# Attention part: value products of two steps together in even steps, projection pieces of two steps together in odd steps, three probability buffers

## What is computed

```python
xn = layernorm(x)                                       # each row
# attention on xn (its own layer norm inside)
q, k, v = proj(Wq, bq), proj(Wk, bk), proj(Wv, bv)      # (8, 16, 1024, 16)
q, k = rope(q), rope(k)
attn = softmax(q @ k.T / sqrt(16))                      # 1024 x 1024 for each of 128 heads
a = xn + (attn @ v).reshape(8, 1024, 256) @ Wo.T + bo
# experts on xn: each of 8 experts takes the 256 rows of a batch with the highest affinity
f = scatter_add(gating * (silu(xs @ Wg) * (xs @ Wu)) @ Wd)
out = x + a + f
```

## Time and profile before

| | us |
|---|---|
| median of 3 runs (2110.39 to 2111.07) | 2110.73 |
| time of the profiled execution | 2107.77 |
| its span, first to last instruction | 2106.2 |
| PE busy | 1842.3 |
| ACT busy | 1197.9 |
| DVE busy | 1113.1 |
| mean granted TensorE clock | 0.949 |

### The profile page before, as it was taken

The page is one execution under the profiler, slowest core; times in us unless marked ns, Lnnn a source line. Parts: engine busy times, 40 slices in busy tenths (PEclk is TensorE's granted clock), DMA queues, the critical chain, the costliest instruction groups (busy, mean ns, idle before and its releaser), DMA issues. The chain is left out here.

```text
span 2106.2 us, 31941 instructions
## 1 busy us (share of the span) xinstructions
PE 1842.3 (87%) x11244; PEld 1004.2 (48%) x11245; DVE 1113.1 (53%) x1904; ACT 1197.9 (57%) x1390; POOL 659.3 (31%) x599
## 2 busy tenths in 40 slices
PE   2469989989989989989989998964999888888997
PEld 2323423423423433334333332224887777777876
DVE  8745446446536536446545558963444444444543
ACT  0058768778778777768867887852333332332331
POOL 3323123123113113212212210001655545455554
PEclk9779999989989999989999999986999999999999
DMA  2255355364363474464464454323433434244333
GB/s 89 84 119 113 94 126 135 103 138 123 100 157 98 116 163 97 126 153 105 127 142 102 127 119 100 77 68 110 88 52 82 76 56 90 45 87 78 55 58 41
DMA packets 115707, 211.63 MB, mean 100 GB/s; under 512 B 17600, under 2 KB 55872, under 8 KB 115520
## 3 DMA queue, kind: packets, MB, share of 16 engines
q1 hardware_dynamic: 84032, 150.33, 29.4%
q0 software_dynamic: 31488, 58.74, 13.6%
HBM read 116.22 MB, written 92.80 MB: 99 GB/s over the span
## 5 line engine op out<-in xcount | busy, mean ns | idle before, releaser
L553 ACT ACTIVATE probs<-score 128x1024 f32<-128x1024 f32 x1024 | 989.0, 1023 | 332.2 <-PE score L708 326.9
L679 PE MATMUL o_ps<-probs,v_ones 128*32 128x512 f32 x4096 | 563.6, 623 | 11.2 <-DVE o_sb L939 10.6
L708 PE MATMUL score<-q_stack,k_stack 50*128 50x512 f32 x2048 | 428.3, 474 | 50.8 <-issue 26.9
L708 PEld LDWEIGHTS score<-q_stack,k_stack 50*128 50x128 f32 x2048 | 184.6, 189 | 308.6 <-issue 166.0
L1220 POOL DMA_INDIRECT out<-y,rows_now x128 | 202.5, 1582 | 268.5 <-DVE y L1372 231.8
L1259 ACT ACTIVATE silu<-g_ps 128x512 f32<-128x512 f32 x128 | 76.5, 598 | 360.9 <-PE g_ps L1293 343.3
L487 POOL TENSOR_TENSOR square<-qk 128x512 bf16<-128x512 f32 x64 | 87.3, 1393 | 475.3 <-DVE qk L858 475.3
L1361 DVE TENSOR_TENSOR h<-u_ps,silu 128x512 f32<-128x512 f32 x128 | 88.5, 692 | 212.3 <-PE u_ps L1293 181.6
L679 PEld LDWEIGHTS o_ps<-probs,v_ones 128*32 128x32 f32 x4096 | 81.6, 109 | 167.7 <-issue 153.2
L1211 POOL DMA_INDIRECT xs<-xn_rows,rows_now x128 | 130.9, 1023 | 47.6 <-issue 29.2
L939 DVE COPY o_sb<-o_ps 128x512 f32<-128x512 f32 x64 | 44.1, 688 | 158.5 <-PE o_ps L679 158.5
(11 more groups left out here) (138 smaller groups left out, 2984.4 us busy)
## 6 DMA issues: line engine op xcount, KB each, us to landing
q_parts<-parts SPq DMA_DIRECT2D x16, 1024.0 KB, 4.4
k_parts<-parts SPq DMA_DIRECT2D x16, 1024.0 KB, 8.2
q_stack<-q_parts SPq DMA_DIRECT2D x64, 256.0 KB, 6.9
k_stack<-k_parts SPq DMA_DIRECT2D x64, 256.0 KB, 8.6
o_sums<-o_sb SPq DMA_DIRECT2D x64, 256.0 KB, 4.8
xin<-in_x POOLq DMA_DIRECT2D x16, 512.0 KB, 5.4
xn_rows<-xn POOLq DMA_DIRECT2D x16, 512.0 KB, 4.9
out<-xin POOLq DMA_DIRECT2D x16, 512.0 KB, 3.4
```

The lines of the kernel that those rows point to most:

```text
L553: act.activation(probs[s % 2][:, 2 * i:2 * i + 2, :], score[i][:, :, :], ACT.Exp, scale=SCALE).then_inc(exp_done[i], 1)
L679: last = pe.matmul(o_ps[j * KEYS_W:(j + 1) * KEYS_W, :], v_ones[par][:, kt, j, :], probs[s % 2][:, j, :], start=kt == 0, stop=kt == KT - 1)
L708: last = pe.matmul(score[i][:, w, :], k_stack[par][rows, i, kt * P:(kt + 1) * P], q_stack[par][rows, i, qh * HALF:(qh + 1) * HALF], start= ...
```

## The change

The order of issue on TensorE changes within each pair of steps (an even and the following odd one). In an even step TensorE issues the scores and then the value products of the two steps before. In an odd step it issues the scores and then all pieces that the tables give to either step of the pair. The tables themselves stay. So pieces of an even step come one step later, and value products of an even step one step later, too. The transposes of affinities at the start of batch 7 stay in step 0, behind the value products. `probs` gets a third buffer; `probs_of` names the buffer of a step, with an extra turn at step 51 so that 64 steps close the cycle, and `steps_since` the distance to the last use of it, which ScalarE's wait on `pv_done` now uses. At the end two steps' value products remain. VectorE, GpSimd and SyncE keep their programs.

```diff
@@ -163,7 +163,7 @@
     q_stack = [sb(f"q_stack{i}", [P, NPAIR, S], F32R) for i in range(2)]
     k_stack = [sb(f"k_stack{i}", [P, NPAIR, S], F32R) for i in range(2)]
     v_ones = [sb(f"v_ones{i}", [P, KT, HPG, KEYS_W]) for i in range(2)]
-    probs = [sb(f"probs{i}", [P, HPG, HALF]) for i in range(2)]
+    probs = [sb(f"probs{i}", [P, HPG, HALF]) for i in range(3)]
     row_max = sb("row_max", [P, HPG * KT])
     neg_max = sb("neg_max", [HPG * KT, P])
     shift = sb("shift", [HPG * KT, NPART, P], F32R)
@@ -237,6 +237,8 @@
                    (39, 40, 41), (42, 43, 44), (45, 46, 47), (48, 49, 50), (56, 57)))
     V_STEPS = ((51, 51, 52), (52, 53, 53), (54, 54, 55), (57, 58, 58))
     PEAK_STEP = (60, 61)
+    EXTRA_STEP = 51
+    assert EXTRA_STEP % 3 == 0 and (STEPS - 1 - EXTRA_STEP) % 3 == 0
     WO_STEPS = ((11, 12, 13), (14, 15, 16), (40, 41, 42), (43, 44, 45))
 
     NORM_STEP, ROUTER_STEP, AFFINITY_STEP = (2, 15), (15, 39), (18, 42)
@@ -250,6 +252,14 @@
     def in_order():
 
         return sorted(((th, k) for th in range(2) for k in range(HJOBS)), key=lambda tk: JOB[tk[0]][tk[1]])
+
+    def probs_of(s):
+
+        return s % 3 if s < EXTRA_STEP else 1 if s == EXTRA_STEP else (s - EXTRA_STEP - 1) % 3
+
+    def steps_since(s):
+
+        return next(n for n in range(1, STEPS) if probs_of((s - n) % STEPS) == probs_of(s))
 
     def need(eng, s, value):
 
@@ -549,8 +559,8 @@
                 for i in range(2):
                     act.wait_ge(qk_done[i], at + 1)
                     if i == 0:
-                        need(act, pv_done, at - 1)
-                    act.activation(probs[s % 2][:, 2 * i:2 * i + 2, :], score[i][:, :, :], ACT.Exp,
+                        need(act, pv_done, at - steps_since(s) + 1)
+                    act.activation(probs[probs_of(s)][:, 2 * i:2 * i + 2, :], score[i][:, :, :], ACT.Exp,
                                    scale=SCALE).then_inc(exp_done[i], 1)
                 if nxt is not None and s in ROUTER_STEP:
                     router(nxt, ROUTER_STEP.index(s))
@@ -677,7 +687,7 @@
                 pe.wait_ge(v_ones_ready, group + 1)
             for j in range(HPG):
                 last = pe.matmul(o_ps[j * KEYS_W:(j + 1) * KEYS_W, :], v_ones[par][:, kt, j, :],
-                                 probs[s % 2][:, j, :], start=kt == 0, stop=kt == KT - 1)
+                                 probs[probs_of(s)][:, j, :], start=kt == 0, stop=kt == KT - 1)
             last.then_inc(pv_done, 1)
 
         def turn_affinities():
@@ -709,29 +719,33 @@
                                          q_stack[par][rows, i, qh * HALF:(qh + 1) * HALF],
                                          start=True, stop=True)
                     last.then_inc(qk_done[i], 1)
-                if s >= 1:
-                    pv(s - 1, b * 2 * NG + (s - 1) // KT, b * NG + (s - 1) // (2 * KT))
-                elif not isinstance(b, int) or b > 0:
-                    pv(STEPS - 1)
+                if s % 2 == 0:
+                    for t in (s - 2, s - 1):
+                        if t >= 0:
+                            pv(t, b * 2 * NG + t // KT, b * NG + t // (2 * KT))
+                        elif not isinstance(b, int) or b > 0:
+                            pv(t + STEPS)
+                    if nxt is None and s == 0:
+                        turn_affinities()
+                    continue
                 if prev is not None:
                     for quarter in range(QUARTERS):
                         for piece, at_step in enumerate(WO_STEPS[quarter]):
-                            if at_step == s:
+                            if at_step // 2 == s // 2:
                                 wo_job(prev, quarter, piece)
                 if nxt is not None:
                     for th in range(2):
                         for k in range(HJOBS):
                             for piece, at_step in enumerate(HALF_STEPS[th][k]):
-                                if at_step == s:
+                                if at_step // 2 == s // 2:
                                     half_job(nxt, th, k, piece)
                     for pair in range(KT // 2):
                         for piece, at_step in enumerate(V_STEPS[pair]):
-                            if at_step == s:
+                            if at_step // 2 == s // 2:
                                 v_job(nxt, pair, piece)
-                    if s in PEAK_STEP:
-                        peak_job(nxt, PEAK_STEP.index(s))
-                elif s == 0:
-                    turn_affinities()
+                    for i, at_step in enumerate(PEAK_STEP):
+                        if at_step // 2 == s // 2:
+                            peak_job(nxt, i)
 
         pe.wait_ge(const_in, CONSTS * DMA)
         pe.wait_ge(weights_split, 1)
@@ -753,6 +767,7 @@
         attend(NB - 1, None, NB - 2)
         for i in range(NPAIR):
             pe.wait_ge(exp_done[i], NB * STEPS)
+        pv(STEPS - 2)
         pv(STEPS - 1)
         for quarter in range(QUARTERS):
             for piece in range(3):
```

## The result

The changed kernel takes 2179.66 us (median of 4 runs, 2173.59 to 2181.26) beside 2110.56 for the kernel before: a ratio of 1.0329, interval 1.0301 to 1.0357, so 3.3% slower. The forecast of 2170 is 10 us short, and the time lies in the range of 2149 to 2203. The same kernel in a second set of four runs gave 2174.4 (ratio 1.0309, 1.0279 to 1.0339). The profiled execution took 2181.13 us, with a mean granted clock of 0.935 where it was 0.949.

What follows compares the result with a forecast made beforehand. TensorE and ScalarE were taken to hold each other in a loop. Six middle batches +43, first batch +8.6, last batch and what follows +12.9, shortened waits -5: +59.5 on the 2110.7 median gave 2170 us, range 2149 to 2203.

Steps and rivals of the forecast that it cites:

- The loop: Each pair: even step's second scores wait for an exponential, two products follow; even step 3.03 us, odd 1.84.
- light: Pairs with at most two transpose or norm pieces, eight a middle batch: from 4.34 to 4.87 us, +4.2 a batch.
- two passes: Pairs with two q/k passes in a middle batch: from 4.66 to 4.87 us each, +1.5 a batch.
- heavy: Middle-batch pairs bound by TensorE's work: minus 0.26 us each from joined products and one entry less, -1.6 a batch.
- peaks: Value-peak transposes in step 61 wait for VectorE's reductions: pair from 4.41 to 5.8 us, +1.4.
- the first four: First four steps of a middle batch, mostly at 1.2 GHz: 12.25 to 14.2 us, +2.0, between +0.5 and +3.5.
- the part behind attention: After the last batch: two value products remain instead of one, +0.9 us.
- A pair cannot take less than 4.87: Floor for every pair of steps: held even step 3.03 us plus odd step at ScalarE's 1.84.
- The second product: Even steps: the added value products cost two pass intervals of 0.455, 0.91 us; bounds 0.87 and 1.00.
- 31 pairs of 4.87: Last batch, without projections: these pairs plus 3.03 and 1.2 for affinity transposes give 155.2 us, +12.0.
- the clock falls in the light stretches: Rival: bare or light pairs at 1.2 GHz take 7.0 us; batch starts +15, all about 90 pairs +190; 5% above 2203.
- the one by which fewer changes of shape make a faster kernel: Rival: TensorE alone sets the pace throughout, some -55 us with the stalls, 2055 us; chance 5%.

Runs made afterwards that it cites:

- experiment 1: Against the changed kernel: value products of two steps still together in even steps, but every projection piece back in its own step; 2319.7 us, ratio 1.0992.
- experiment 2: Against the changed kernel: one step's value products in every step as before, all pieces of two steps still in odd steps; 2199.4 us, ratio 1.0421.
- experiment 4: Against the changed kernel: in even steps the older of the two products stands between the two score pairs; 2153.6 us, ratio 1.0206.
- Experiment 5: Against the changed kernel: eight unused filler matmuls of 256 columns in batch 7's odd steps without output pieces, from step 3; 2156.8 us, ratio 1.0225.
- selective kernels: Against the kernel before: products and pieces joined only in selected pairs, one output piece moved, three probability buffers; four variants, 2106.35, 2104.0, 2106.4 and 2117.7 us.
- experiments 6 to 10: The four selective kernels (6, 8, 9, 10), 2104.0 to 2117.7 us, and 7: the changed kernel with step 43's output piece behind its q/k pieces, 2170.7 us.

## Why the prediction was right, and where it was off

**The loop, right.** Even step 3.03 forecast, 2.99 measured; odd 1.84 and 1.82; pair 4.87 and 4.82. A gap of 1.05 stands before each run of four exponentials of the light pairs (1.1 forecast), and sixteen product records in a row, as written down. Experiments 1, 2 and 4 change the amount and the place of the work behind the release and leave the sum on TensorE alike but for one or two entries a pair; the length of the held steps follows the place each time. That the forecast of pairs was made in parts can be checked on the means of batches 2 to 5, before and after:

| pair (first step) | before | after | forecast of the difference |
|---|---|---|---|
| 0 and 2 | 11.86 | 13.18 | +2.0 |
| 4, 6 (light) | 8.67 | 11.52 | +1.06 |
| 28 (light) | 4.33 | 4.83 | +0.53 |
| 22 (two passes) | 4.65 | 4.82 | +0.21 |
| 40 (heavy) | 5.60 | 5.34 | -0.26 |
| 42 (heavy) | 5.59 | 6.38 | -0.26 |
| 60 (peaks) | 4.42 | 5.73 | +1.4 |
| 62, with the loop's end | 9.12 | 9.00 | +0.7 |

The middle batches together grew by 34.5 where 38 was said, the first by 10.0 where 8.6 was. That the sum comes so near is partly luck. By kinds of pair, in us a batch (batches 2 to 5), with the forecast in brackets: eight light +5.7 (+4.2), seven with two passes +0.2 (+1.5), six heavy -0.2 (-1.6), seven between -1.4 (-1.1), peaks +1.3 (+1.4), the last two steps -0.1 (+0.7), the first four +1.3 (+2.0). The errors cancel for the most part. In the whole they do so too, in part: against its forecast batch 7 came 21 us over, batches 1 to 6 3.5 under and the part behind attention 6.3 under.

**The floor, too general.** "A pair cannot take less than 4.87" fails for pairs 18, 46 and 56, which take 4.37, 4.34 and 4.40 after the change. Their even steps last 2.52 to 2.54, TensorE's own 0.67 and 1.85: each follows an odd step that TensorE's work made long, so that no exponential is left to hold the second scores. The prediction knew this for step 62 alone ("now not held by ScalarE"), where it shows as 2.52. It is why the pairs with two passes cost less than was said.

**The second product, mis-sized.** Priced at 0.91 from the interval between two passes, it costs 0.85. I had taken the interval as the difference of two record lengths, whose ends are modelled; back to back a pass takes 0.425 (half of 0.85). My lower bound of 0.87 was too high as well. At 0.05 a pair this is about 12 us less over the 250 pairs.

**The last batch, wrong step.** "31 pairs of 4.87" and 3.03: the term is wrong for fourteen of the 32 even steps, step 62 among them. In these the clock fell in the products, 22.2 us. I had this as a rival ("the clock falls in the light stretches"), with the argument that an even step of 3.03 stays busy for nine tenths. The step that failed is this: I looked at the busy step and not at the odd one before it, in which TensorE idles 0.88 and 0.42 us around a score pair. The price was near (7.0 for such a pair, measured 4.65 + 1.82 = 6.5: only the products run slow), but I put it to the starts of batches and to all light pairs, while it came to about half of the bare pairs. The starts have it too: pairs 4 and 6 of the middle batches take 1.95 and 0.90 longer in place of 0.53. Experiment 5 shows the cause: with only this idle time filled the clock stays up.

**A wait that I missed.** Step 43 lasts 3.86 us, steps with the same pieces 2.75. Timeline of step 43 after:
```profile
742.48 0.40 PE L656 MATMUL wo_ps<-w_lo,at_hi 128*128 128x256 f32 x2
...
742.92 0.69 DVE L979 TENSOR_TENSOR base<-wo_ps,base 128x512 f32<-128x512 f32 x1 [3.10 <-PE wo_ps L656]
...
743.75 0.48 PE L656 MATMUL wo_ps<-w_hi,at_hi 128*128 128x256 f32 x2 [0.87 <-DVE base L979]
...
745.87 1.94 ACT L563 ACTIVATE probs<-score 128x1024 f32<-128x1024 f32 x2 [1.92 <-PE score L718]
```
The last piece of the third quarter (step 42) and the first of the fourth (step 43) now stand back to back, and both use `wo_ps`: VectorE must add the one before TensorE may write the other. I had this pair as "minus 0.26". It lost 0.79 in each of the middle batches; in the last, without q/k pieces, step 43 takes 2.92 in place of 1.82. This is the reader's check for any merge of steps: which pairs of pieces share a buffer that a third engine has to empty between them.

**Peaks, right in the mechanism.** 5.73 where 5.8 was said: the second pair of transposes waits for VectorE's reductions, which start behind its last addition to v_sb and take 4.48 us.
```profile
785.25 4.48 DVE L888 TENSOR_REDUCE peaks<-v_sb 128x1 f32<-128x2048 f32 x2
...
788.03 0.38 PE L644 MATMUL side<-ident_sb,peaks 128*1 128x128 f32 x2
...
789.78 0.38 PE L644 MATMUL side<-ident_sb,peaks 128*1 128x128 f32 x2 [1.37 <-DVE peaks L888]
```
The parts were sized otherwise: the odd step lasts 2.72 and not 3.2 (the wait is 1.37, not 1.9), and the 0.45 that the next even step gives back falls into pair 62, which so loses nothing where +0.7 was said.

**The part behind attention, not foreseen.** It is 5.4 us shorter. The traces say where: counted from the first exponential of the last step, the first output piece starts at 12.0 us in the kernel before and at 6.9 in the changed one, and the last output piece ends at 39.3 and 34.7. VectorE's reciprocal of the sums, on which the first piece depends, comes 0.1 us behind that exponential before, and 6.3 ahead of it after. That VectorE gets there sooner because batch 7, in which it also picks the top rows, is 33 us longer was not tested.

**The rule on tiling modes, weighed.** Of the rivals, the one by which fewer changes of shape make a faster kernel is refuted for held pairs: the change has fewer than the kernel before and is slower, and in experiment 4 light pairs with two more changes are 0.35 shorter. In pairs that TensorE's sum bounds it holds: 5.60 to 5.34 us for pair 40 with the change, and 5.60 again in experiment 4. The Trainium skill, page "TensorEngine Tiling (Array Packing)", section on tiling modes, says that a change of mode drains TensorE; the traces agree that something is lost (1.00 against 0.85 for a product), and show that it counts only where nothing holds the scores.

## What to carry to other kernels

When two engines hand each other small buffers in a ring, and one issues in order, cost a reordering by what stands behind each released instruction until the next handover, not by busy time: work bunched behind one release makes a gap on the partner that a lighter step cannot give back, since the partner has a floor of its own. Work that does not depend on the release can stand in front of it: that shortened held pairs by 0.35 us and made the others 0.30 longer (experiment 4). Bunching saved about 0.3 us in pairs whose sum exceeds the floor, but the selective kernels lost that again elsewhere (experiments 6 to 10). Price the clock by the idle time in a whole period, the light step included.

## What the runs showed of the hardware that was not expected

- In a periodic pattern of 4.82 us in which TensorE idled 0.88 and 0.42 us, the granted clock fell to 1.2 GHz in fourteen of 32 periods, for the products above all, which took 3.60 us in place of 1.92, and was back at 2.4 GHz for the next scores (0.73). With idle stretches of 0.30 and 0.41 us (light pairs) or of about 0.2 (the filler), or with one of 0.89 in a period of 4.47 (experiment 4), it stayed up in nearly all. In experiment 1, whose light pairs idle 0.52 and 0.41 us in 5.19, it fell in 12 of the 28 pairs of steps 28 to 35 (even steps of 4.95 to 5.03 in place of 3.37).
- Useless matmuls in idle time made a kernel 17.6 us faster.
- TensorE's branch at the end of the loop's body takes 5.2 to 6.8 us in the four selective kernels (medians of 5.7 to 6.1) and 3.3 to 5.3, mostly under 4.6, in the others with as many instructions, in another order.
